# A two-layer vision tower on one core: embedding with centred weights, scores of two heads in one product, softmax and FFN steps in another order

## What is computed

```python
embedded = patches(x) @ Wp + bp                      # K = 768, six blocks of 128
position = relu(xy @ W1 + b1) @ W2 + b2
h = embedded + position
h = h + attn0(ln(h))         # 8 heads whose keys and values are shared
h = h + gated_ffn(ln(h))     # returns ln(h) plus, for 31 of 64 tokens ranked by ln(h) @ wr, the gated output
h = h + attn1(ln(h))         # 8 heads of 8, bias from an edge table
h = h + moe(ln(h))           # returns ln(h) plus the top 2 of 8 experts
```

## Time and profile before

| | |
|---|---|
| median of 3 runs | 72.43 us (72.35 to 72.58) |
| the profiled execution's own time | 72.43 us |
| its span (first to last instruction) | 70.6 us |
| PE busy | 62.7 us, 89% |
| DVE, ACT, POOL busy | 41.8, 29.2, 13.5 us |
| granted TensorE clock, mean | 1.000 |
| DMA | 4.07 MB, mean 58 GB/s |

### The profile page before, as it was taken

The page is one execution under the profiler, slowest core; times in us unless marked ns, Lnnn a source line. Parts: engine busy times, 40 slices in busy tenths (PEclk is TensorE's granted clock), DMA queues, the critical chain, the costliest instruction groups (busy, mean ns, idle before and its releaser), DMA issues.

```text
span 70.6 us, 1972 instructions
## 1 busy us (share of the span) xinstructions
PE 62.7 (89%) x830; PEld 38.7 (55%) x830; DVE 41.8 (59%) x108; ACT 29.2 (41%) x63; POOL 13.5 (19%) x32
## 2 busy tenths in 40 slices
PE   3996996999999999998979996979999978999940
PEld 1330563778798577364424575458695327664910
DVE  2491099675699992824961537989673015756830
ACT  0340103413678833257852515158703374863030
POOL 6800096000000990076304000000000004000000
PEclk9999999999999999999999999999999999999999
DMA  0799999910000000000000000000000000000003
GB/s 1 176 382 389 381 244 264 271 64 0 0 9 0 0 0 9 0 0 5 0 0 0 0 0 9 0 0 9 0 0 9 5 0 0 0 0 0 0 0 74
DMA packets 2389, 4.07 MB, mean 58 GB/s; under 512 B 779, under 2 KB 1229, under 8 KB 2381
## 3 DMA queue, kind: packets, MB, share of 16 engines
q1 hardware_dynamic: 1568, 3.49, 16.5%
q10 hardware_dynamic: 781, 0.46, 2.2%
q0 software_dynamic: 32, 0.00, 0.0%
HBM read 3.82 MB, written 0.13 MB: 56 GB/s over the span
## 4 chain that ended last, share of the span: by engine, by line
PE 66%; DMA 9%; DVE 7%; ACT 6%; issue 3%; POOL 3%; DVEq 0%; ACTq 0%; POOLq 0%
DMA Xt<-in_x_dram 9%; PE psum L693 9%; PE psum L687 6%; POOL WoS L297 3%; PE psum L703 3%; PE psum L914 3%; PE psum L899 3%; PE psum L945 3%; PE psum L795 3%; PE psum L997 3%; PE psum L746 3%; ACT E L377 2%; PE psum L1037 2%; PE psum L722 2%; PE psum L859 2%
## 5 line engine op out<-in xcount | busy, mean ns | idle before, releaser
L693 PE MATMUL psum<-warm 128*128 128x512 bf16 x54 | 17.4, 437 | 1.2 <-DVE warm L462 1.2
L693 PEld LDWEIGHTS psum<-warm 128*128 128x128 bf16 x54 | 5.3, 108 | 7.0 <-issue 3.6
L297 POOL TENSOR_TENSOR WoS<-pack_attn,top 128x256 f32<-128x256 f32 x5 | 3.1, 649 | 11.0 <-DVE top L517 11.0
L475 DVE TENSOR_TENSOR onehot<-idb,iota 128x2048 bf16<-128x2048 bf16 x4 | 4.8, 1242 | 0.0
L332 POOL TENSOR_TENSOR resT<-hT,xC 128x256 f32<-128x256 f32 x1 | 0.7, 724 | 20.7 <-DVE xC L637 20.7
L411 ACT ACTIVATE E<-E 128x512 f32<-128x512 f32 x4 | 2.5, 630 | 3.4 <-DVE E L608 3.4
L354 ACT ACTIVATE lv<-psum,eps 128x256 f32<-128x256 f32 x4 | 1.9, 475 | 3.5 <-PE psum L735 0.9
L606 DVE TENSOR_REDUCE top<-psum 128x8 f32<-128x512 f32 x4 | 2.7, 685 | 0.6 <-PE psum L914 0.6
L914 PE MATMUL psum<-kT,qT 9*64 9x64 f32 x128 | 2.1, 231 | 1.1 <-DVE qT L594 0.7
L440 ACT ACTIVATE ge<-psum,pack_moe 128x512 f32<-128x512 f32 x4 | 2.5, 688 | 1.2 <-PE psum L997 1.2
L779 PE MATMUL psum<-top,pack_ident 128*128 128x256 f32 x12 | 2.9, 388 | 0.0
(11 more groups left out here) (202 smaller groups left out, 131.9 us busy)
## 6 DMA issues: line engine op xcount, KB each, us to landing
Xt<-in_x_dram SPq DMA_DIRECT2D x1, 1024.0 KB, 6.3
Xt<-in_x_dram SPq DMA_DIRECT2D x1, 512.0 KB, 7.5
pack_both<-in_both_dram SPq DMA_DIRECT2D x2, 240.2 KB, 8.6
pack_moe<-in_moe_dram SPq DMA_DIRECT2D x1, 450.0 KB, 9.3
pack_mid<-in_mid_dram SPq DMA_DIRECT2D x1, 327.5 KB, 9.2
pack_attn<-in_attn_dram SPq DMA_DIRECT2D x1, 288.0 KB, 7.8
pack_expert<-in_expert_dram SPq DMA_DIRECT2D x2, 130.0 KB, 9.0
pack_wp<-in_wp_dram ACTq DMA_DIRECT2D x1, 192.0 KB, 5.8
```

Source lines behind the costliest of these rows:

```text
L297: gp.tensor_tensor(WoS[:, s, 4 * u:4 * u + 4, :].rearrange("p (b n) d -> p b n d", b=2), bc(WoT[:, 2 * u:2 * u + 2, :], 1, 2), bc(top0[:, ...
L475: ve.tensor_tensor(onehot[:, 16 * k:16 * k + 16, :], bc(idb[:, k, :], 1, 16), iota16[:, :, :], ALU.is_equal).then_inc(s_hot, 1)
L693: mm(B[bank][:, :], lhsT=warm[:, 0:P], rhs=warm[:, :], start=True, stop=True)
```

## The change

1. *Embedding centred.* DVE computes `Wpc = Wp - mean over its 64 columns` and the same for the position weights (`posc`), so that PE's embedding products give the centred stream directly, in B[1]. The position part goes first, with the images after it. ACT squares straight from B[1] and copies it to hT[0] behind the square. The centring product of the first norm is gone. Wp is issued first on SP's queue instead of second on ACT's.
2. *Token mean.* The mean that the stream now lacks is formed by six groups of products (`token_mean`, in B[3], in places where `keep_clock` stood) and a position part, copied to `meanT` by ACT and added on POOL (`hM`) before the last residual sum.
3. *Order up to the queries.* The four one-hots stand behind the centring in DVE's queue and `centre` behind them; the head matrices are split around the product of the squares; four clock-keeping products are gone; the last 16 edge products run behind the values.
4. *Scores of two heads in one product.* 64x128 weights (two heads) instead of 64x64: eight products a slot instead of 16. q0 is laid out so that two heads of 64 tokens are adjacent.
5. *Softmax.* Slot 1's shift goes ahead of slot 3's scores; slot 0's sum and reciprocal are taken in two halves, ahead of slot 3's maximum; POOL scales both halves of slot 1, ACT's four copies move to slot 2, DVE keeps one product (slot 3).
6. *FFN.* The rank product goes between the two halves of the output product; hidden tiles move to banks 0, 1, 4, 5, router weights to bank 2.
7. *Keys.* K's third tile goes to bank 1, and DVE starts on the first when it is ready instead of after the third.

```diff
+            load(pack["wp"][:, :], packs["wp"], in_wp)
             load(Xt[:, :, 0:4, :], packs["x"][:, :, 0:4, :], in_x[0])
             load(Xt[:, :, 4:6, :], packs["x"][:, :, 4:6, :], in_x[1])
...
-            scaled_Wo(2)
-            scaled_Wo(3)
+            pool.wait_ge(s_wsum, 3)
...
+            scaled_Wo(0, 0, 1)
+            scaled_Wo(0, 1, 2)
+            scaled_Wo(1, 0, 3)
+            scaled_Wo(1, 1, 3)
+            scaled_Wo(2, 0, 4)
+            scaled_Wo(3, 1, 5)
...
+            pool.wait_ge(s_hm_ev, 1)
+            pool.wait_ge(s_h2, 1)
+            gp.tensor_tensor(hM[:, :], hT[2][:, :], meanT[:, :], ALU.add).then_inc(s_h2, 1)
...
-            act.dma_start(pack["wp"][:, :], packs["wp"]).then_inc(in_wp, 16)
...
+                if k == 0:
+                    sc.activation(hT[0][:, :], HC[:, 0:HALF], ACT.Copy).then_inc(s_h, 1)
...
-            act.wait_ge(s_emb, 1)
-            sc.activation(hT[0][:, :], B[0][:, 0:HALF], ACT.Copy).then_inc(s_h, 1)
             deviation(0)
...
-            ins.then_inc(s_exp0, 1)
+            for u in range(2):
+                for i in range(4 * u, 4 * u + 4):
+                    ins = sc.activation(E0[:, 0, i, :], B[i // 4][:, i % 4 * TOK:(i % 4 + 1) * TOK], ACT.Exp,
+                                        bias=shift[:, i:i + 1], scale=SC0)
...
             for s in range(1, SLOTS):
                 act.wait_ge(s_sub0, s)
                 sc.activation(E0[:, s, :, :].rearrange("p (m q) t -> p m (q t)", m=2), psum[:, 2 * s:2 * s + 2, 0:HALF],
                               ACT.Exp, scale=SC0).then_inc(s_exp0, 1)
-            act.wait_ge(s_rinv, 2)
+            mixed(0)
+            act.wait_ge(s_rinv, 4)
             for i in range(4, HEADS):
-                ins = sc.activation(WoS[:, 1, i, :], WoT[:, 2 + i % 2, :], ACT.Copy, scale=top0[:, 2, 1, i:i + 1])
+                ins = sc.activation(WoS[:, 2, i, :], WoT[:, 2 + i % 2, :], ACT.Copy, scale=top0[:, 2, 2, i:i + 1])
             ins.then_inc(s_wosa, 1)
-            mixed(0)
             mixed(1)
...
             sc.preload_act_table_set("natural_log_exp_and_others")
             deviation(2)
+            act.wait_ge(s_hm, 1)
+            sc.activation(meanT[:, :], B[3][:, 0:HALF], ACT.Copy).then_inc(s_hm_ev, 1)
...
+            def centred(dst, src, sums, n):
+                ve.tensor_reduce(sums, src, X, ALU.add).then_inc(s_wsum, 1)
+                dve.wait_ge(s_wsum, n)
+                ve.scalar_tensor_tensor(dst, bc(sums, len(src.shape) - 1, D), -1.0 / D, src, ALU.mult, ALU.add).then_inc(s_wpc, 1)
+
+            dve.wait_ge(in_pos, 16)
+            centred(posc[:, :].unsqueeze(1), posW2.unsqueeze(1), wsum[0:D + 2, KX:KX + 1], 1)
+            dve.wait_ge(in_wp, 16)
+            centred(Wpc[:, 0:2, :], Wp[:, 0:2, :], wsum[:, 0:2], 2)
+            centred(Wpc[:, 2:KX, :], Wp[:, 2:KX, :], wsum[:, 2:KX], 3)
             hot(0)
+            hot(1)
+            hot(2)
+            hot(3)
             dve.wait_ge(in_ident, 16)
             dve.wait_ge(s_blk, 3)
             ve.tensor_tensor(centre[:, :], ident, mean64[:, :], ALU.subtract).then_inc(s_centre, 1)
-            hot(1)
-            hot(2)
-            hot(3)
 
             def normal(k):
...
-            dve.wait_ge(s_expo, 4)
-            ve.tensor_scalar(expo[:, :, :], B[0][:, 0:2 * TOK].bitcast(i32).rearrange("p (j u) -> p j u", u=2),
-                             23, None, ALU.logical_shift_right).then_inc(s_expo_ev, 1)
             for u in range(2):
                 dve.wait_ge(s_q0, 2 * u + 2)
-                ve.tensor_copy(q0[:, 1, 2 * u:2 * u + 2, :], B[6 + u][:, :].rearrange("p (q t) -> p q t", q=2)).then_inc(s_q0_v, 1)
+                ve.tensor_copy(q0[:, 1, :, 2 * u:2 * u + 2, :].rearrange("p b q t -> p q b t"),
+                               B[6 + u][:, :].rearrange("p (q b t) -> p q b t", q=2, b=4)).then_inc(s_q0_v, 1)
+                if u == 0:
+                    dve.wait_ge(s_expo, 4)
+                    ve.tensor_scalar(expo[:, :, :], B[0][:, 0:2 * TOK].bitcast(i32).rearrange("p (j u) -> p j u", u=2),
+                                     23, None, ALU.logical_shift_right).then_inc(s_expo_ev, 1)
...
             softmax0_max(2)
+            for u in range(2):
+                dve.wait_ge(s_exp0h, u + 1)
+                softmax0_sum(0, slice(4 * u, 4 * u + 4), u + 1)
             softmax0_max(3)
-            softmax0_sum(0)
             for s in range(1, SLOTS):
-                softmax0_sum(s)
-            for s, u in ((2, 1), (3, 0)):
-                dve.wait_ge(s_rinv, s + 1)
...
                                      ALU.add).then_inc(s_q1_v, 1)
                 for g in range(2):
+                    dve.wait_ge(s_k1, ((1, 3), (4, 4))[c][g])
+                    bank = 1 if c == 0 and g == 1 else 5 + 2 * c
                     ve.tensor_tensor(kT1[:, g, c * HALF:(c + 1) * HALF].rearrange("p (b n) -> p b n", n=TOK),
-                                     B[5 + 2 * c][:, g * HALF:(g + 1) * HALF].rearrange("p (b n) -> p b n", n=TOK),
...
-            pe.wait_ge(s_centre, 1)
-            pe.wait_ge(s_h, 1)
-            mm(B[1][:, 0:HALF], lhsT=centre[:, :], rhs=hT[0][:, :], start=True, stop=True).then_inc(s_hc, 1)
...
+            pe.wait_ge(in_pos, 16)
+            mm(B[4][0:D, 0:P], lhsT=posW1, rhs=grid, start=True, stop=True).then_inc(s_posh, 1)
+            pe.wait_ge(s_wpc, 1)
+            pe.wait_ge(s_posh_ev, 1)
+            pe.wait_ge(s_warm, 2)
+            for c in range(2):
+                mm(B[1][rows[c], 0:HALF], lhsT=posc[:, :], rhs=bc(posh[:, :], 1, 2), start=True, stop=False)
+            pe.wait_ge(s_wpc, 3)
+            pe.wait_ge(in_x[0], 16)
+            for q in range(4):
+                embed(q)
+            pe.wait_ge(in_x[1], 16)
+            embed(4)
+            embed(5).then_inc(s_hc, 1)
+            pe.wait_ge(in_attn0, 16)
+            head_products(0)
+            head_products(1)
+            pe.wait_ge(s_blk, 3)
             pe.wait_ge(s_sq, 1)
             mm(B[2][:, 0:HALF], lhsT=mean64[:, :], rhs=sq[0][:, :], start=True, stop=True).then_inc(s_var, 1)
-            keep_clock(3, 2)
-            for k in range(4):
+            head_products(2)
+            head_products(3).then_inc(s_g, 1)
+            for k in range(3):
                 last_rows(k)
-            keep_clock(3, 2)
             pe.wait_ge(s_x, 1)
             pe.wait_ge(s_g_ev, 2)
...
+            last_rows(3)
...
                         for m in range(2):
-                            for k in range(2):
-                                src = xC[0] if m == c else xS
-                                last_mm = s == 0 and n == 1 and b == 1
-                                ins = mm(B[2 * s + m][rows[k], col:col + TOK], lhsT=q0[rows[m], c, 2 * n + k, tok],
-                                         rhs=src[rows[m], tok], start=(n == 0 and b == 0), stop=last_mm, skip_group_check=True)
+                            ins = mm(B[2 * s + m][:, col:col + TOK], lhsT=q0[rows[m], c, 2 * j + b, 2 * n:2 * n + 2, :],
+                                     rhs=(xC[0] if m == c else xS)[rows[m], tok], start=(n == 0 and b == 0),
+                                     stop=(s == 0 and n == 1 and b == 1), skip_group_check=True)
                 ins.then_inc(s_sc0, 1)
...
             scores0(2)
+            shift0(1)
             scores0(3)
-            shift0(1)
             shift0(2)
             shift0(3)
+            pe.wait_ge(s_exp0h, 2)
+            keep_clock(0, 1)
+            mix0(0)
             pe.wait_ge(s_exp0, 1)
-            keep_clock(0, 3)
-            mix0(0)
-            pe.wait_ge(s_exp0, 2)
-            keep_clock(2, 1)
+            pe.wait_ge(s_wmean, 2)
+            for c in range(2):
+                mm(B[3][rows[c], 0:HALF], lhsT=wmean[0:D + 2, KX:KX + 1].broadcast_to([D + 2, D]), rhs=bc(posh[:, :], 1, 2),
+                   start=True, stop=False, skip_group_check=True)
             mix0(1)
             out0(0)
...
+            token_mean(0)
+            pe.wait_ge(s_centre, 1)
             pe.wait_ge(s_h, 2)
             mm(B[7][:, 0:HALF], lhsT=centre[:, :], rhs=hT[1][:, :], start=True, stop=True).then_inc(s_hc, 1)
-            keep_clock(2, 2)
+            token_mean(1)
...
             for k in range(2):
                 for c in range(2):
...
                     ins = mm(B[6][rows[c], 0:HALF], lhsT=w2f[:, k, :], rhs=hid[:, k, c * HALF:(c + 1) * HALF], start=False,
                              stop=(k == 1))
-            ins.then_inc(s_y, 1)
+                return ins
+
+            ffn_out(0)
             pe.wait_ge(const_l1, 1)
             pe.wait_ge(s_cmp, 1)
+            pe.wait_ge(s_gelu, 2)
             for c in range(2):
                 ins = mm(B[5][rows[c], 0:HALF], lhsT=ones_h[rows[c], :], rhs=ahead_h[rows[c], :, :].rearrange("p b n -> p (b n)"),
                          start=True, stop=True)
             ins.then_inc(s_rank, 1)
+            ffn_out(1).then_inc(s_y, 1)
             pe.wait_ge(s_res, 1)
...
```

(20 more changed lines are left out.)

120 lines of the change are left out of this document (60 added, 60 removed).

## The result

| | before | after |
|---|---|---|
| median of 4 runs each, taken in turn | 72.47 us (72.35 to 72.58) | 78.23 us (73.96 to 81.81) |
| ratio | | 1.027, 95% interval 1.016 to 1.039 |
| span of the profiled execution | 70.6 us | 72.1 us (its time 73.96) |
| mean granted TensorE clock | 1.00 (profiled run) | 0.976, 0.977, 0.914, 0.915 (its four runs) |

The change makes the kernel slower. The forecast was 71.5 us, the range 70.6 to 72.9: wrong in sign, and outside the range. The four runs of after are 73.96, 74.92, 81.55 and 81.81 us, and the last two are those with the granted clock at 0.91.

A forecast was written before the change was run, and what follows sets the result against it. PE was taken to hold two thirds of the chain, then the image DMA. From 72.43 us, attention's end -0.65, token mean +0.15, K -0.05 and FFN -0.4 sum to -0.95: 71.5 us, range 70.6 to 72.9.

The forecast's parts named there:

- images at 7.33 and products 0.13 later, 7.46: Image load: 130 KB more beside the images at 394 GB/s delays landing 0.33 us from 7.00; embedding starts at 7.46.
- clock rival: Embedding: PE nearly idle from 5.5 to 7.46 drops to 1.2 GHz, up to 3.0 us more, 73 to 74; chance 0.07.
- Position pack at 4.9, Wpc at 7.0: Before the embedding: position pack lands at 4.9 us (bounds 3.8 and 7.0), centring takes 2.1, ready at 7.0.
- late-pack rival: Before the embedding: PE's start hangs on the position pack; break-even landing 5.8, at 7.0 the kernel takes 73.6; chance 0.16.
- Square at 10.6: End of embedding: 24 products take 3.1 us, so the square starts at 10.6 against 12.17, 1.6 earlier.
- Square to queries 2.85: Before the queries: DVE late with one-hots, G's copies and normalization until 13.4; queries start at 13.45 instead of 15.85.
- Queries to scores 3.12: Before the scores: queries and values 2.36, moved edge products 0.40, exponent extraction 0.35; scores start at 16.57.
- Slot 0.86, first maximum 1.1 after the scores: Attention scores: eight steps of 0.107, 0.86 us a slot, 0.34 slower; first maximum at 17.67 against 18.99.
- rival of instruction-bound scores: Attention scores: instruction count sets the slot at 0.26 us, first maximum 0.6 earlier, time 70.6; chance 0.10.
- First maximum to last output product 9.6: Attention softmax and mix: DVE and POOL late, 9.6 us against 8.9, giving back 0.7.
- Changes of the array's shape at zero: PE tile shapes: changes cost nothing; at 0.33 us each, two on the path would make 72.1 instead of 71.5.
- From the last output product to the end -0.30: Behind attention: token mean +0.15, K's evacuation -0.05, FFN order -0.4 us.

The follow-up runs named there:

- b_wpfirst: Kernel before with only the Wp pack moved ahead of the images on SP's queue: 76.77 us against 72.95, ratio 1.048.
- b_order: Kernel before with only the new softmax order, one head per product: 73.22 us against 72.78, ratio 1.005.
- a_xfirst_fill: Changed kernel with images first on SP, Wp on ACT behind the position pack, four filling products before the embedding: 73.42, 78.1, 79.84 and 100.88 us.
- b_w14: Kernel before with 14 first clock-keeping products instead of 12: 72.56 us, none of 12 runs low in clock.
- b_best_w14: Kernel before with FFN order, K's first tile early, four clock-keeping products around the edge products gone, 14 first products: 71.63 us against 72.78, ratio 0.981.
- b_warm8: Kernel before with 8 instead of 12 clock-keeping products ahead of the embedding: 75.43 us, ratio 1.032.
- a_fill: Changed kernel with four more clock-keeping products between the position product and the wait for the images: 73.85 us against 72.95, ratio 1.011.
- b_rest: Kernel before with the changed scores, softmax, FFN and K order, no clock-keeping around edge products, 14 first products; old embedding: 72.55 us against 72.53, ratio 0.999.
- a_fill_sc64: Changed kernel with four filling products before the embedding and scores back to one head per product: 72.93 us, ratio 0.999.
- a_fill8: Changed kernel with eight filling products between the position part and the embedding: 74.64 us, five of 12 runs low in clock.

## Why the prediction was wrong

**The step that failed is "images at 7.33 and products 0.13 later, 7.46".** They landed at 8.38, and the embedding began at 8.52. The step names Wp's issue ahead of the images and puts it at nothing, though they are issued 0.44 us later; it prices bytes only, and too few: 130 KB at 394 GB/s. The windows show 0.31 MB more ahead of the landing (0.8 us) and two microseconds in which the engines moved 0.27 MB less (0.7 us); b_wpfirst, with the one line moved in the kernel before, has them at 8.9. The edge ids, in the same place of ACT's queue as before, took 2.9 us in place of the 1.9 of the earlier trace rows, which tells the same. The Trainium skill ("DMA: Bandwidth & Descriptors", Issuing engines are not separate DMA queues) says that transfers of all issuing engines run on the same 16 DMA engines and interleave. The trace agrees as far as it goes: the order of issue on one queue changes what has moved by the time the images are there, 1.97 MB in place of 1.65. Why more goes ahead, and why the engines pause, was not tried.

**The clock rival was the one that came**, at a chance of 0.07 and "73 to 74"; the profiled run is 73.96, and the two runs of 81.6 lie far beyond its price. It was argued down with waits of 0.5 us, though the prediction itself saw PE nearly idle from 5.5 to 7.46; with the landing at 8.38 that became 1.85 us of nothing. (That the loss isn't certain with such a wait, b_order shows.) The Trainium skill ("TensorE: Matmul & The Clock Gate", Part 1) has PE at 1.2 GHz after idleness and at 2.4 GHz when busy, and the trace agrees, with 24 products in 4.30 us against 3.03. What no row of before could show is that the level, once lost, may last to 21 us.

**Against the forecast's steps.** The forecast's span is 71.5 - 1.83 = 69.67, and the profiled one 72.1, 2.4 more:
- Position pack at 4.9, Wpc at 7.0: right (its reduction starts at 5.17, the last Wpc ends at 6.95). The late-pack rival falls.
- Square at 10.6: 12.86, **+2.26**. Images 1.06, the failed step; embedding 4.34 in place of 3.14, 1.20, the lost level.
- Square to queries 2.85: 2.81, right in number, but not for the reason given. The forecast had DVE late there, its one-hots and G's copies, by a hair. In after the one-hots end at 11.59, DVE waits 2.74 us for PE's head products before it copies G, and the queries follow the scale and the edge products. In a_xfirst_fill, where Wp comes late, DVE is indeed what the queries wait for.
- Queries to scores 3.12: 3.34, +0.2. PE idles 0.43 (the "issue" at 18.58) until DVE has extracted the exponents of the 16 products moved behind the values.
- Slot 0.86, first maximum 1.1 after the scores: 0.89 and 1.15, right. The rival of instruction-bound scores (0.26) falls, with the rule that the prediction names beside it.
- First maximum to last output product 9.6: 9.86, +0.26. That attention would give back time was right; that DVE and POOL would be what is late was not: PE is full from 19.01 to 25.94 in the chain, and POOL isn't in it; 0.8 us of the loss is there before the first mix. That two different limits come out within 0.3 us is luck.
- Changes of the array's shape at zero: the chain shows no gap from the values to the edge products (17.66 + 0.43, then 18.10), and none at the FFN's; the one from the edge products to the scores is hidden in the 0.43 just named.
- From the last output product to the end -0.30: 42.08 against 42.71, -0.63. xC[1] to yG -0.38 as forecast (-0.4); of the rest 0.24 is a pause in the profiled run of before among the maxima of attention 1 (the third starts 1.59 us after the second, in after 1.32). Such a pause stands in b_w14, b_best_w14, b_warm8 and b_wpfirst too, and in none of the changed kernels; its cause is open.

Take away the 2.26 of the late images and the lost level, and the sum comes to 71.7, beside the 71.5 forecast. That is closer than the steps are: +0.22 and +0.26 stand against -0.33, most of it the pause. And it would still have been too good as a forecast of this idea: a_fill, with the level held in six runs of eight, is 73.85, since the second piece of the images is late as well, and b_rest shows that outside the embedding the parts sum to nothing.

## What to carry to other kernels

Before a load is put ahead of the one that the first long stage waits for, change that order alone in the old kernel and time it: here it cost 4.8%, late landing and lost level together, more than any other part. An idle stretch of TensorE is priced with what follows it, since the level can be lost in it and may come back late; look at how far apart products start, not at the granted clock only. Work that is put ahead in a queue brings its wait along: slot 1's shift ahead of slot 3's scores, meant to start slot 1 sooner, left PE idle for 0.42 us where one head per product leaves room for it.

## What the runs showed of the hardware that was not expected

- The granted clock may read 1.00 while products run at half pace: b_warm8, eight in 1.97 us, as the first twelve of the earlier trace rows do.
- The low level can outlast the return of work by far: 12 us in b_wpfirst with PE busy most of the time, 3 us in after.
- The same waits can end at either level. PE idles 1.86 us in b_order, and eight products then take 1.08; 1.85 in after, and they take 1.97. a_fill and a_fill_sc64 run the same first products with the same waits, and at 6.63 the position products take 0.65 in one and 1.12 in the other.
- The same program's runs fall on steps of mean clock (1.00, 0.977, 0.954, then 0.93 and less); in the kernel before the first three are 72.2 to 73.2, 74.2 to 75.0 and 75.6 to 76.3 us.
- With a 192 KB pack ahead of them on the queue the images land 8.4 to 9.6 us after the span's start, when 2.0 to 2.4 MB have moved; with the images first at 6.4 to 7.5, with 1.4 to 1.8 MB. In after the DMA engines also had pauses (share 0.69 and 0.71 from 3 to 5 us; in before 0.85 and 0.97), which b_wpfirst and a_fill8 hardly have (0.91).
